# Reordering the end of a mixture-of-experts layer: shared pair last, two VectorE low parts, high products first

## The reference, cut to what matters

```python
scores = sigmoid(x @ router_w.T)                 # x: 1024 tokens x 128, layer-normed
# grouped top-k: 8 of 64 experts for each token, weights w * 2.5, zero elsewhere
coef = zeros((T, E)).at[arange(T)[:, None], topk_idx].add(topk_w)
g = einsum('th,ehi->tei', x, Wg)                 # 64 experts, H = 128, I = 64
u = einsum('th,ehi->tei', x, Wu)
h = silu(g) * u * coef[:, :, None]
moe_out = einsum('tei,eih->th', h, Wd)
shared = silu(x @ SWg) * (x @ SWu) @ SWd         # I_SH = 128, no coefficient
return moe_out + shared
```

## Time and profile before

| | |
|---|---|
| median of 3 runs | 302.14 us (302.12 to 302.27) |
| the profiled execution's own time | 301.8 us |
| its span, first to last instruction | 300.0 us |
| granted TensorE clock, mean | 1.000 |
| matmuls (PE) | 286.9 us busy, 96% of the span |
| VectorE (DVE), ScalarE (ACT), GpSimd (POOL) | 76%, 64%, 62% |

### The profile page before, as it was taken

The page is one execution under the profiler, slowest core; times in us unless marked ns, Lnnn a source line. Parts: engine busy times, 40 slices in busy tenths (PEclk is TensorE's granted clock), DMA queues, the critical chain, the costliest instruction groups (busy, mean ns, idle before and its releaser), DMA issues.

```text
span 300.0 us, 5440 instructions
## 1 busy us (share of the span) xinstructions
PE 286.9 (96%) x1721; PEld 204.2 (68%) x1721; DVE 228.2 (76%) x511; ACT 192.6 (64%) x354; POOL 184.9 (62%) x259
## 2 busy tenths in 40 slices
PE   8999989999999999899979999999999999999994
PEld 3665756666665655465655788888888888888883
DVE  3797897799678877988894759889966666666664
ACT  2887857877885666567553788666564655555553
POOL 8430070297509872974187699999965665665661
PEclk9999999999999999999999999999999999999999
DMA  7722364458485341350002536665433343344411
GB/s 254 251 29 45 122 197 112 114 158 235 86 220 101 79 110 64 90 141 2 2 1 43 186 133 202 217 198 176 136 101 127 117 166 131 116 140 134 125 59 35
DMA packets 30636, 37.18 MB, mean 124 GB/s; under 512 B 5136, under 2 KB 19856, under 8 KB 30608
## 3 DMA queue, kind: packets, MB, share of 16 engines
q1 hardware_dynamic: 30608, 36.84, 42.6%
HBM read 28.43 MB, written 3.93 MB: 108 GB/s over the span
## 4 chain that ended last, share of the span: by engine, by line
PE 77%; DVE 11%; POOL 5%; issue 2%; ACT 2%; DMA 1%; ACTq 0%; DVEq 0%; POOLq 0%
PE bank L487 54%; PE bank L865 5%; PE bank L867 5%; PE bank L866 5%; DVE rawmax L1303 2%; POOL stacks L1832 2%; PE bank L691 2%; PE bank L673 1%; PE bank L648 1%; DMA xres<-x 1%; PE bank L493 1%; PE bank L660 1%; PE bank L696 1%; POOL xn L306 1%; POOL stacks L1838 1%
## 5 line engine op out<-in xcount | busy, mean ns | idle before, releaser
L1868 POOL TENSOR_TENSOR qbd<-vs,qbd 128x512 fp32r<-128x512 f32 x65 | 83.5, 1287 | 33.5 <-ACT qbd L1180 33.4
L487 PE MATMUL bank<-khl,stacks 128*128 128x512 f32 x396 | 101.5, 392 | 1.8 <-DVE vs L1663 1.8
L487 PEld LDWEIGHTS bank<-khl,stacks 128*128 128x128 f32 x396 | 73.6, 188 | 18.7 <-issue 3.7
L1694 DVE TENSOR_TENSOR conv<-bank,conv 128x512 f32<-128x512 f32 x60 | 41.5, 691 | 31.4 <-ACT bank L1144 28.1
L1144 ACT ACTIVATE bank<-bank 128x512 f32<-128x512 f32 x61 | 35.5, 582 | 43.9 <-PE bank L487 43.9
L1303 DVE TENSOR_REDUCE rawmax<-bank 128x4 f32<-128x512 f32 x64 | 43.2, 684 | 8.7 <-PE bank L487 7.8
L1180 ACT ACTIVATE qbd<-vs 128x512 fp32r<-128x512 f32 x65 | 40.7, 625 | 7.1 <-DVE vs L1671 4.6
L1702 DVE TENSOR_TENSOR vs<-conv,bank 128x512 f32<-128x512 f32 x61 | 41.9, 687 | 2.1
L487 PE MATMUL bank<-stacks 128*128 128x512 f32 x96 | 41.2, 477 | 1.1 <-DVE stacks L1613 0.6
L1062 ACT ACTIVATE conv<-bank 128x512 f32<-128x512 f32 x64 | 35.2, 596 | 7.6 <-PE bank L487 6.9
L1832 POOL TENSOR_TENSOR stacks<-ring,stacks 128x384 fp32r<-128x384 f32 x33 | 33.6, 1018 | 1.4
(11 more groups left out here) (240 smaller groups left out, 439.0 us busy)
## 6 DMA issues: line engine op xcount, KB each, us to landing
conv<-coefficient_rows SPq DMA_DIRECT2D x122, 128.0 KB, 2.9
ring<-w SPq DMA_DIRECT2D x33, 192.0 KB, 3.5
stacks<-stacks SPq DMA_DIRECT2D x68, 64.0 KB, 2.1
split_rows<-stacks SPq DMA_DIRECT2D x6, 256.0 KB, 2.4
stacks<-split_rows SPq DMA_DIRECT2D x16, 96.0 KB
split_rows<-khl SPq DMA_DIRECT2D x3, 512.0 KB, 4.3
stacks<-split_rows SPq DMA_DIRECT2D x8, 192.0 KB
pa<-pack_a SPq DMA_DIRECT2D x1, 706.0 KB, 5.3
```

What stands on the lines that cost most here:

```text
L487: return pe.matmul(out, lhsT, rhs, start=start, stop=stop)
L1694: dve.tensor_tensor(out, gate, spread[:, n % ROWS, :, :], ALU.mult).then_inc(gate_scaled, 1)
L1868: pool.tensor_tensor(hlo[:, n % 4, :].rearrange("p (b t) -> p b t", b=4), hx[n % 4], hhi[:, n % 4, :].bitcast(F32).rearrange("p (b t) -> p ...
```

## The change

In the second half the order of pairs is 1 to 32 and then 0 (`pair_of`). Unit 33 therefore needs coefficients, and unit 65, now the shared pair, needs none: VectorE's scaling in `last_unit()` is gone. GpSimd no longer forms the low part of unit 64; VectorE does, before its two for unit 65. TensorE adds the two products of `hhi` for units 64 and 65 first (`down_high`), then the product of `hlo` for unit 64, and then that of unit 65 in two pieces (`down_low`).

```diff
+        def pair_of(n):
+            return n if n < PER_HALF else (n + 1) % PER_HALF
...
-            before = n // ROWS - 1 - (1 if n > PER_HALF and n % ROWS == PER_HALF % ROWS else 0)
+            before = n // ROWS - 1
...
-                e0 = 2 * (n - PER_HALF * c) - 2
+                e0 = 2 * pair_of(n) - 2
...
-            for n in range(FIRST, UNITS):
-                if n == PER_HALF + 1:
+            for n in range(FIRST, UNITS - 1):
+                if n == PER_HALF:
                     rows_out(1)
-                if n != PER_HALF:
-                    coefficient_rows(n)
+                coefficient_rows(n)
...
+            def down_high(n):
+
+                w, pair = n % 4, pair_of(n)
+                for weights in (whi(pair), wlo(pair)):
+                    pe.matmul(bank[1][:, :], weights[:, 2, :], hhi[:, w, :], start=False, stop=False,
+                              skip_group_check=True)
+
+            def down_low(n, cols, stop):
+
+                return pe.matmul(bank[1][:, cols], whi(pair_of(n))[:, 2, :], hlo[:, n % 4, cols], start=False, stop=stop,
+                                 skip_group_check=True)
...
-            for n in range(UNITS - 1 + LAG):
+            for n in range(UNITS - 2 + LAG):
                 unit(n)
+            pe.wait_ge(hhi_ready, UNITS - 1)
+            down_high(UNITS - 2)
+            pe.wait_ge(hhi_ready, UNITS + 1)
+            down_high(UNITS - 1)
+            pe.wait_ge(last_hlo, 1)
+            down_low(UNITS - 2, slice(0, HALF), False)
             for i in range(2):
-                pe.wait_ge(last_hlo, i + 1)
-                down(UNITS - 1, slice(2 * P * i, 2 * P * i + 2 * P))
+                pe.wait_ge(last_hlo, i + 2)
+                last = down_low(UNITS - 1, slice(2 * P * i, 2 * P * i + 2 * P), True)
+            last.then_inc(down_done, 1)
...
-                act.wait_ge(down_done, UNITS + 1)
+                act.wait_ge(down_done, UNITS - 1)
...
-                if n % PER_HALF == 0:
-                    dve.tensor_copy(out, gate).then_inc(gate_scaled, 1)
-                else:
-                    dve.wait_ge(ld_c[n % ROWS], spread_in(n))
-                    dve.tensor_tensor(out, gate, spread[:, n % ROWS, :, :], ALU.mult).then_inc(gate_scaled, 1)
+                dve.wait_ge(ld_c[n % ROWS], spread_in(n))
+                dve.tensor_tensor(out, gate, spread[:, n % ROWS, :, :], ALU.mult).then_inc(gate_scaled, 1)
...
                 for i in (0, 2):
-                    two = slice(4 * p + i, 4 * p + i + 2)
                     dve.wait_ge(silu_done, n + 1 + i // 2)
-                    dve.tensor_tensor(scaled[:, two, :], sg[:, two, :], spread[:, n % ROWS, i:i + 2, :],
-                                      ALU.mult).then_inc(gate_scaled, 1)
-                    dve.wait_ge(gate_scaled, n + 1 + i // 2)
-                    dve.tensor_tensor(hx[w][:, i:i + 2, :], scaled[:, two, :], four(4 + p)[:, i:i + 2, :],
-                                      ALU.mult).then_inc(h_done, 1)
+                    dve.tensor_tensor(hx[w][:, i:i + 2, :], sg[:, 4 * p + i:4 * p + i + 2, :],
+                                      four(4 + p)[:, i:i + 2, :], ALU.mult).then_inc(h_done, 1)
+                dve.wait_ge(hhi_ready, n)
+                dve.wait_ge(down_done, n - 4)
+                low_product(n - 1, 0, 4)
+                dve.wait_ge(down_done, n - 3)
                 for i in (0, 2):
-                    cols = slice(P * i, P * i + 2 * P)
                     dve.wait_ge(hhi_ready, n + 1 + i // 2)
-                    dve.tensor_tensor(hlo[:, w, cols].rearrange("p (b t) -> p b t", b=2), hx[w][:, i:i + 2, :],
-                                      hhi[:, w, cols].bitcast(F32).rearrange("p (b t) -> p b t", b=2),
-                                      ALU.subtract).then_inc(last_hlo, 1)
+                    low_product(n, i, 2)
...
-            for n in range(UNITS - 1):
+            for n in range(UNITS - 2):
                 unit(n)
```

More of the change, by code:

```diff
@@ L829, in products @@
             def products(n, of=(0, 1)):
-                c, p, pair = n // PER_HALF, n % 2, n % PER_HALF
+                c, p, pair = n // PER_HALF, n % 2, pair_of(n)
                 xh, xl = xhl[:, 0, HALF * c:HALF * c + HALF], xhl[:, 1, HALF * c:HALF * c + HALF]
@@ L859, in _, with down @@
                 accumulate_residual(b)
[L861 to L867, removed]
-                          skip_group_check=True).then_inc(down_done, 1)
+            def down(n):
+                w, pair = n % 4, pair_of(n)
+                acc, stop = bank[n // PER_HALF][:, :], n == PER_HALF - 1
+                pe.matmul(acc, whi(pair)[:, 2, :], hhi[:, w, :], start=False, stop=False, skip_group_check=True)
+                pe.matmul(acc, whi(pair)[:, 2, :], hlo[:, w, :], start=False, stop=False, skip_group_check=True)
+                pe.matmul(acc, wlo(pair)[:, 2, :], hhi[:, w, :], start=False, stop=stop,
+                          skip_group_check=True).then_inc(down_done, 1)
+            def down_high(n):
+                w, pair = n % 4, pair_of(n)
+                for weights in (whi(pair), wlo(pair)):
[4 more added lines that the diff above has]
+                                 skip_group_check=True)
             def unit(n):
@@ L900, in unit @@
                     products(5)
-                if LAG <= n < UNITS - 1 + LAG:
+                if n >= LAG:
                     pe.wait_ge(hlo_ready, n - LAG + 1)
-                    down(n - LAG, slice(0, HALF))
+                    down(n - LAG)
                 if n == 5:
@@ L1702, in unit, with low_product @@
                 dve.tensor_tensor(hx[n % 4], scaled[:, 4 * p:4 * p + 4, :], four(4 + p), ALU.mult).then_inc(h_done, 1)
+            def low_product(n, b, blocks):
+                cols = slice(P * b, P * b + P * blocks)
+                dve.tensor_tensor(hlo[:, n % 4, cols].rearrange("p (b t) -> p b t", b=blocks), hx[n % 4][:, b:b + blocks, :],
+                                  hhi[:, n % 4, cols].bitcast(F32).rearrange("p (b t) -> p b t", b=blocks),
+                                  ALU.subtract).then_inc(last_hlo, 1)
             def last_unit():
```

## The result

The changed kernel takes 300.67 us (median of 22 runs, 300.27 to 302.89) against 302.12 us before (22 runs beside them, 301.69 to 304.05): a ratio of 0.9958, 95% interval 0.9941 to 0.9974. It was forecast at 300.66 us. The interval is wide because the executions of either kernel lie on two levels 1.7 to 1.9 us apart, a difference outside the change, to which the last experiments return; on the lower level the medians are 300.49 and 302.07 us, 1.58 us apart.

The account below looks back on a forecast made before the run. TensorE was taken as the bound, busy 96% of the span, except for waits after the last products. Removing two waits of 0.74 us each gave 302.14 - 1.48 = 300.66 us, range 300.3 to 301.3.

Parts of the forecast that it names:

- The end, engine by engine: After unit 65's up factor: TensorE never waits and its last matmul starts at 295.19, not 296.67, 1.48 us less.
- Rival 1: Last stretch: unit 64's low part takes 1.28 us and low parts become the bound; gain 1.17 us, 300.97; chance 0.22.
- Rival 2: Last stretch: ScalarE's high parts of unit 65 reach TensorE late; gain under 0.6 us, about 301.7; chance 0.07.
- Rival 3: Middle: unit 33's coefficient rows land late; at 8 us late 2.0 us slower, 304.2; chance 0.03.
- The 3.0 us of the prediction: Slack between unit 33's scaling at 227.18 and TensorE's gate product of unit 35 near 230.2, behind 1.5 us of cover.
- a wait of 0.74 us: TensorE's wait for unit 64's low part (293.94 to 294.68) goes, and 0.74 us of waits and small steps behind it.
- The rule on the shared reads: VectorE operations with two SBUF inputs contend with GpSimd's SBUF reads, the later blocked wholly; costs nothing once GpSimd is done.

Follow-up runs that it names:

- the last experiments: Changed kernel with its two groups of single-column matmuls apart (300.25 to 300.78 us), or each followed by an added 512-column matmul (301.99 to 302.56 us).
- f_low_twice: Changed kernel with VectorE forming unit 64's low part twice in a row; 301.11 us on the lower level, 301.37 us median of all executions.
- e_rows_late: Changed kernel with unit 33's coefficient rows held back until unit 32 is scaled, 2.5 us late; 300.64 us.
- e_rows_later: Changed kernel with unit 33's coefficient rows held back until unit 34's up products are done, 6 us late; 303.60 us on the lower level, 305.25 us median.
- a_pairs: Changed kernel with TensorE's and GpSimd's part put back, so only the pair order differs from before; 301.42 us on the lower level, 301.52 us median.
- c_pool: Changed kernel with unit 64's low part back on GpSimd; 300.77 us on the lower level, 301.01 us median.
- after_again: The changed kernel itself, run again as control; twelve executions, six on the upper level, median 301.38 us.
- d_order: Changed kernel with TensorE's matmuls for units 64 and 65 in the old order, low parts on VectorE; 300.86 us on the lower level, 301.05 us median.

## Why the prediction was right

**The end, engine by engine: right.** TensorE was to run from unit 63's last matmul to the end without a wait and save 1.48 us; the tail is 1.49 us shorter, and the lower level 1.58. The five VectorE rows were forecast at 0.42, 0.42, 0.69, 0.42 and 0.42 us; the trace has 0.42 twice on L1737 and 0.69 and 0.42 twice on L1725. Set back by the 0.35 us of this execution, its output copy starts at 295.50, where the prediction had it near 295.5. That the medians agree to 0.01 us is luck. The lower level fell by 0.10 more than the 1.48, which the tail doesn't show and no run explains, and the median of the changed kernel was raised by ten of 22 executions on the upper level, against seven of 22 before.

**Rival 1, the low parts as the bound: not so, but near.** The room of the last low part was forecast at 0.34 us before the hand-over, and f_low_twice finds 0.3 with the hand-over counted. The unknown duration of the low part at 512 columns was 0.69, as its neighbours had it.

**Rival 2: excluded by the trace.** ScalarE's three roundings of units 64 and 65 follow each other within 1.4 us (292.99 to 294.37), and TensorE takes the high products without a gap.

**Rival 3, the slower side: the place was right.** Unit 33 doesn't wait for its rows in the change, but for silu:

```profile
226.84 0.69 DVE L1712 TENSOR_TENSOR conv<-bank,conv 128x512 f32<-128x512 f32 x1 [0.63 <-ACT bank L1165]
```

e_rows_late and e_rows_later bracket the slack behind that wait: 2.5 us cost nothing, 6.0 us cost 3.3. The 3.0 us of the prediction was 2.7; it had left out the 0.14 us from the end of the scaling to TensorE's start (233.28 to 233.42 in e_rows_later).

**Which part earned what.** The prediction split the gain into a wait of 0.74 us and as much behind it. The experiments split it by edit: pair order alone 0.58, the rest alone 0.73, both 1.49, so 0.18 us comes only with both. The wait of 0.74 us before unit 64 is still whole in a_pairs, which gains only behind it. In the changed kernel the order of the matmuls is worth 0.40 and the move to VectorE 0.24. The move is worth that although VectorE does more for it, because its own low parts then no longer meet GpSimd: the first one's 1.12 us is the only row of the last stretch that is stretched in c_pool.

**The rule on the shared reads: right.** VectorE's operations with two SBUF inputs took 1.28 (before), 1.10 (a_pairs) and 1.12 us (c_pool) beside GpSimd and 0.42 without, while the one with a PSUM input took 0.42 beside it. The Trainium skill, "SBUF — State Buffer", section "Who interferes with whom", has the later one blocked wholly. The trace agrees nearly: all three ended 0.28 to 0.29 us after GpSimd's operation, two thirds of their full 0.42.

**What I had not allowed for** is the second level: the range of 300.3 to 301.3 holds the lower one, and the median only because more than half of the executions lay on it. In after_again, the same kernel, half of twelve did, and the median was 301.38 us, outside the range.

## What to carry to other kernels

In a pipeline that ends on one engine, write down that engine's last operations and for each the latest of its inputs: put those with early inputs first, and let the unit with the shortest way be the last. Before moving work between VectorE and GpSimd, look for VectorE operations with two SBUF inputs that run at the same time; the meeting can cost more than the work (here 0.86 us on an operation of 0.42). When two executions differ by more than the change should, compare the length of the stretch that was changed, and look at the granted clock of the rest.

## What the runs showed of the hardware that I had not expected

TensorE's granted clock fell to 0.50 (1.2 GHz) behind 16 rows of single-column matmuls in 1.9 us, in some executions and not in others of the same kernel, and the six float32 rows behind took 4.33 instead of 2.82 us. With those 16 in two groups, the second convolution of 2.8 us between them, none of 14 executions lay on the upper level. Why a given execution falls or not stays open, and so does the shorter fall near 40 to 44 us (0.15 us in the profile after), which no run here tried to remove.

A matmul of 512 or 256 columns costs 0.227 or 0.12 us in a row without waits, but the first after a wait is followed only 0.34 or 0.22 us later, and if it is the last, it ends 0.1 us later: a wait costs TensorE some 0.1 us beyond its own length. The rows of the weight loads (PEld) show one difference. In a row without waits a matmul's load starts 0.23 us ahead of it (294.06 for 294.29 in the profile after); in d_order the load and the matmul behind the wait both start at 294.14. That this is where the 0.1 us comes from is an inference, and no run tests it.
